# Column sums in column form, other instruction orders and two groups of constant products in an attention and ternary feed-forward kernel

## The chip, the cores and the metric

The kernel runs on one core of a Trainium2 chip. The metric is the device time of one execution in microseconds, as the median of three runs. The profile is one further execution, with its own time.

## The reference

For x of shape (8, 512, 256), each row is normalized (`xn`), and the output is `x + attention(xn) + ffn(xn)`. The core of it:

```python
q, k, v = split_heads(xn @ Wq), split_heads(xn @ Wk), split_heads(xn @ Wv)   # 16 heads of 16
scores = einsum('bhld,bhlwd->bhlw', q, k_win) * scale                        # window of 64 keys
ctx = einsum('bhlw,bhlwd->bhld', softmax(scores), v_win)
attention = ctx @ Wo

h = gelu(einsum('btd,hd->bth', xn, absmean(W_fc)))        # weights become -1, 0 or 1
h = layernorm(h, ln_w, ln_b)                              # over 1024 hidden values
ffn = einsum('bth,dh->btd', h, absmean(W_proj))
```

The layernorm is folded into the second product: with T the ternary `W_proj`, the kernel needs the two vectors of 256 sums `sum_h ln_w[h] T[d,h]` and `sum_h ln_b[h] T[d,h]`. The first is multiplied by each row's mean, the second is added to every row.

## The kernel before, in words

The eight batches go through the same jobs on TensorE (PE), each job ending in one semaphore. A job is named (batch, kind, number). Per batch there are: `xt` (8 transposes of xn), `qk` 0 and 1 (the q and k products, 12 of 512 columns each), `v` (24 of 256 columns), `fc` 0 to 3 (8 of 512 columns each), `sa` 0 to 7 (scores for the row maxima), `mt` (transposes of the maxima), `st` 0 to 7 (scores transposed, for the exponentials), `gt` 0 to 3 (8 transposes of the gelu output each), `proj` 0 to 3 (16 of 256 columns each), `pv` 0 to 7, `ct` 0 and 1 and `wo` 0 to 3. `sa` and `st` work on half of the array's rows at a time and begin with products that add the window mask from `mask_q`, `mask_k` and `onehot`; `sa` 0 of a batch is the first that reads the masks and the stacked copies of q and k.

PE takes the jobs in the order of the list ORDER, which is FIRST, then PERIOD repeated, then LAST, written out by hand as tables. Batches overlap: the exponentials and attention products of one batch stand between the q, k, fc and score jobs of the next. Results go to two rings of PSUM buffers, `big` (3 buffers: xt, qk, v, fc, sa, st, gt) and `small` (2 buffers, all others). A job waits until the job three (or two) places before it in its ring has been read out.

The other engines have orders of their own, written as lists of calls. ScalarE (ACT) rounds results to fp16 (`xt_hi`, `qk_split`, `g_hi`, `ct_hi`), does gelu (`gel`) and the exponentials (`probs`, `p_parts`). VectorE (DVE) makes the remainders (`xt_lo`, `qk_split`, `g_lo`, `ct_lo`), the maxima `negmax` (`maximum`, line 1016), the statistics of the hidden layer (`hidden_statistics`), and the sums of outputs. GpSimd (POOL) makes constants, masks and fillings at the start, and the remainders of the exponentials (`lower_part`, line 578). SyncE (SP) issues the DMAs: q and k go through `load_stack` as 12 DMAs per batch (line 374), the masks are copied to the second half of the partitions by `copy_masks` (lines 411 and 412).

The start of the program, on which much of the prediction rests:

- ACT sums |W_fc| (`absolute`, line 789); PE spreads the sum over the partitions (`sums`, line 1640). DVE takes the weights' maxima (line 1086), PE transposes them (`wmax`, line 1633), DVE writes `diag` (`largest`, lines 1096 and 1098), PE spreads it (`spread`, line 1636), and DVE makes scales from it.
- `xt` of batch 0 (line 1501), then DVE's `xt_lo` (line 992) and the 24 products of `qk` (line 1513).
- POOL fills `k_stack` with four memsets (lines 597 and 598).
- `crow` (line 1649): 48 products of 256 columns, with one column of `lnv_parts` as the stationary operand and T as the moving one. They leave the two vectors of sums in one row; `copy_row` (line 1152) copies it to `crow`, `csum` (line 1655) spreads it to 128 partitions, and `copy_sums` (line 1156) copies it to SBUF. POOL's `residual` and `add_mean` read it.

A batch's `gelu` t waits for the `hidden_statistics` t of the batch before.

Of the kernel before, what the change touches and what calls it, by code (L numbers as in the profile page):

```python
# [5 lines left out]
def attention_and_ternary_ffn(  # L6
# [53 lines left out]
    with ctx:  # L60
# [26 lines left out]
        crow = sb("crow", [1, 2 * D], fp32)  # L87
# [173 lines left out]
        def sig(name):  # L261
# [4 lines left out]
        FIRST = [(0, "wmax", 0), (0, "spread", 0), (0, "sums", 0), (0, "wmax", 1), (0, "xt", 0), (0, "spread", 1),  # L266
# [23 lines left out]
        PERIOD = [(3, "st", 0), (2, "pv", 6), (4, "fc", 0), (2, "ct", 0), (4, "fc", 1), (4, "fc", 2), (4, "fc", 3),  # L290
# [6 lines left out]
        LAST = [(5, "st", 0), (4, "pv", 6), (6, "fc", 0), (4, "ct", 0), (6, "fc", 1), (6, "fc", 2), (6, "fc", 3),  # L297
# [408 lines left out]
        def _(act):  # L706
# [91 lines left out]
            weight_upper(1)  # L798
            qk_upper(0, 1)
            gelu(0, 0)  # L800
            gelu(0, 1)
            gelu(0, 2)
            v_upper(0)
            normalize(1)
# [894 lines left out]
```

## Time and profile before

| | us |
|---|---|
| median of 3 runs | 398.52 |
| lowest and highest run | 396.35, 399.64 |
| profiled execution, its own time | 397.85 |
| its span, first to last instruction | 396.0 |
| PE busy | 373.7 (94%) |
| DVE busy | 321.2 (81%) |
| ACT busy | 287.6 (73%) |
| POOL busy | 231.4 (58%) |

The time of an execution is its span and 1.85 us around it. Matmuls are pipelined in the records: each lasts longer than the distance to the next. A wait on PE that is shorter than this overlap doesn't show as idle time, so the work on PE is read from the starts of the instructions and not from their durations.

### The profile page before, as it was taken

Reading aid. Unit: us, or ns where it says so; the run is one execution under the profiler, and the core shown is the slowest. Engines: PE = TensorE matmul, PEld = TensorE weight load, DVE = VectorE, ACT = ScalarE, POOL = GpSimd, SP = SyncE. Lnnn points to the kernel's source line nnn. Section 1 sums busy time; section 2 is a strip of 40 time slices with the busy share of each in tenths; the row PEclk is TensorE's granted clock in tenths of the full one; section 3 lists DMA queues with packets and bytes.
Section 4 is the critical chain, followed back from the end, with each engine's and each line's share of the span. In section 5 each row is a group of like instructions: output and inputs, shape, how many; then the busy total and the mean of one; then the engine's idle time right before and its main releaser. Section 6 shows DMA issues by size and latency. Waiting matters only on the chain.

```text
span 396.0 us, 13503 instructions
## 1 busy us (share of the span) xinstructions
PE 373.7 (94%) x5820; PEld 268.1 (68%) x5820; DVE 321.2 (81%) x645; ACT 287.6 (73%) x329; POOL 231.4 (58%) x186
## 2 busy tenths in 40 slices
PE   0698898999999999999999999999999999999995
PEld 0346565776577776876677775876677775778873
DVE  3898878699869998699959898599968898998555
ACT  2764249887986698767986698777977598768871
POOL 7901023866586548655576548655576647769871
PEclk9999989999999999999999999999999999999999
DMA  7459009600940267021910258021930256002002
GB/s 272 153 78 123 2 10 181 87 19 5 165 51 18 48 125 134 2 65 33 198 30 18 48 116 142 4 63 33 190 38 17 52 97 109 2 17 66 30 29 82
DMA packets 30685, 29.22 MB, mean 74 GB/s; under 512 B 5665, under 2 KB 29281, under 8 KB 30625
## 3 DMA queue, kind: packets, MB, share of 16 engines
q1 hardware_dynamic: 30624, 28.35, 36.6%
q8 instruction: 46, 0.75, 0.9%
q14 instruction: 15, 0.11, 0.1%
HBM read 7.35 MB, written 4.19 MB: 29 GB/s over the span
## 4 chain that ended last, share of the span: by engine, by line
PE 85%; DMA 4%; DVE 4%; ACT 3%; SPq 2%; issue 1%; POOL 1%; POOLq 1%; ACTq 0%
PE small L1600 15%; PE big L1539 13%; PE big L1513 11%; PE small L1611 10%; PE big L1590 7%; PE big L1578 5%; PE big L1553 5%; PE big L1525 5%; PE small L1627 5%; PE big L1583 4%; PE big L1559 4%; DMA mask_k<-mask_k 2%; SPq L374 2%; DMA gel<-in_w_fc 2%; PE small L1617 2%; PE big L1501 2%
## 5 line engine op out<-in xcount | busy, mean ns | idle before, releaser
L578 POOL TENSOR_TENSOR p_parts<-probs,p_parts 128x1024 f16<-128x1024 f32 x64 | 136.2, 2132 | 112.8 <-ACT p_parts L762 112.8
L761 ACT ACTIVATE probs<-big,exp_scale 128x1024 f32<-128x1024 f32 x64 | 71.4, 1116 | 22.9 <-PE big L1583 20.7
L1016 DVE TENSOR_REDUCE negmax<-big 128x8 f32<-128x1024 f32 x64 | 77.6, 1222 | 7.1 <-PE big L1559 5.7
L762 ACT ACTIVATE p_parts<-big,exp_scale 128x1024 f16<-128x1024 f32 x64 | 71.3, 1115 | 0.0
L1600 PE MATMUL small<-proj_t,g_hi 128*128 128x256 f16 x256 | 57.7, 273 | 0.0
L1600 PE MATMUL small<-proj_t,g_lo 128*128 128x256 f16 x256 | 57.5, 273 | 0.0
L776 ACT ACTIVATE g_hi<-big,lnw_s 128x512 f16<-128x512 f32 x64 | 39.8, 690 | 17.2 <-PE big L1590 17.2
L1539 PE MATMUL big<-fc_t,xt_hi 128*128 128x512 f16 x128 | 48.5, 379 | 1.0 <-DVE g_lo L1010 1.0
L1539 PE MATMUL big<-fc_t,xt_lo 128*128 128x512 f16 x128 | 48.6, 379 | 0.0
L1010 DVE SCALAR_TENSOR_TENSOR g_lo<-big,lnw_s,g_hi 128x512 f16<-128x512 f32 x64 | 46.5, 746 | 2.2 <-ACT g_hi L776 1.8
L749 ACT ACTIVATE gel<-big 128x1024 f32<-128x1024 f32 x32 | 32.7, 1025 | 12.6 <-PE big L1539 12.2
L1052 DVE SCALAR_TENSOR_TENSOR y_bufs<-small,rs,res 128x256 f32<-128x256 f32 x32 | 15.5, 483 | 30.6 <-PE small L1600 27.5
L1063 DVE TENSOR_TENSOR ctxn<-small,rden 64x128 f32<-64x128 f32 x128 | 36.9, 288 | 3.1
L1590 PE MATMUL big<-ident,gel 128*128 128x128 f32 x256 | 33.7, 280 | 0.0
L731 ACT ACTIVATE qk_split<-big 128x1024 f16<-128x1024 f32 x16 | 16.4, 1023 | 19.6 <-PE big L1513 19.1
L559 POOL TENSOR_TENSOR res<-x_in,csum 128x1024 f32<-128x1024 f32 x8 | 18.9, 2357 | 19.2 <-issue 19.2
L1590 PEld LDWEIGHTS big<-ident,gel 128*128 128x128 f32 x256 | 28.7, 143 | 1.5 <-DVE g_lo L1010 0.2
L1583 PEld LDWEIGHTS big<-q_stack,k_stack 50*128 50x128 f16 x1024 | 23.9, 94 | 7.6
L1553 PE MATMUL big<-mask_q,onehot 64*64 64x512 bf16 x256 | 26.0, 395 | 2.5 <-DMA mask_k<-mask_k 1.9
L1600 PEld LDWEIGHTS small<-proj_t,g_hi 128*128 128x128 f16 x256 | 25.0, 97 | 3.6
L1600 PEld LDWEIGHTS small<-proj_t,g_lo 128*128 128x128 f16 x256 | 25.0, 98 | 2.8
L1559 PEld LDWEIGHTS big<-k_stack,q_stack 48*64 48x64 f16 x1024 | 22.2, 106 | 6.3
(130 smaller groups left out, 812.2 us busy)
## 6 DMA issues: line engine op xcount, KB each, us to landing
q_stack<-qk_split SPq DMA_DIRECT2D x48, 128.0 KB, 4.0
k_stack<-qk_split SPq DMA_DIRECT2D x48, 128.0 KB, 5.3
x_in<-in_x SPq DMA_DIRECT2D x8, 512.0 KB, 5.5
out<-y_bufs SPq DMA_DIRECT2D x32, 128.0 KB, 2.4
v_odd<-v_even SPq DMA_DIRECT2D x16, 132.0 KB, 2.5
v_odd<-v_even SPq DMA_DIRECT2D x16, 99.0 KB, 2.2
gel<-in_w_fc SPq DMA_DIRECT2D x1, 1024.0 KB, 6.7
y_bufs<-in_w_proj SPq DMA_DIRECT2D x1, 1024.0 KB, 8.8
```

The costliest lines, as they stand in the source:

```text
L578: g.tensor_tensor(p_lo[:, (b * NJ + j) % PB], probs[:, (b * NJ + j) % PB], p_hi[:, (b * NJ + j) % PB], ALU.subtract).then_inc(*sig(p_lo_re ...
L761: s.activation(probs[:, (b * NJ + j) % PB].rearrange("p i (u q) -> p u i q", u=2), st, ACT.Exp, scale=exp_scale[:, 0:1]).then_inc(*sig(exp ...
L762: s.activation(p_hi[:, (b * NJ + j) % PB].rearrange("p i (u q) -> p u i q", u=2), st, ACT.Exp, scale=exp_scale[:, 0:1]).then_inc(*sig(p_hi ...
L776: s.activation(g_hi[:, i], slot[b, "gt", i // 2][:, i % 2], ACT.Copy, scale=lnw_s[:, i:i + 1]).then_inc(*sig(g_hi_ready))
L1010: v.scalar_tensor_tensor(out=g_lo[:, i], in0=slot[b, "gt", i // 2][:, i % 2], scalar=lnw_s[:, i:i + 1], in1=g_hi[:, i], op0=ALU.mult, op1= ...
L1016: v.tensor_reduce(negmax[:, :, j], slot[b, "sa", j][:].rearrange("p a (u k) -> p (a u) k", k=P), AX.X, ALU.max, negate=True).then_inc(*sig ...
L1513: last = mm(ps[:, m], wt[pw][:, n, k, m * P:(m + 1) * P], xt[px][:, k], start=(i == 0), stop=(i == 3 * KD - 1))
L1539: last = mm(ps[:, a], xt[px][:, k, n * P:(n + 1) * P], fc_t[:, k, a * L:(a + 1) * L], start=(i == 0), stop=(i == 2 * KD - 1))
L1553: mm(ps[a * W:(a + 1) * W, u], onehot[rows, a], mask_q[rows, 1 if n == 0 else 0].rearrange("p u k -> p (u k)"), start=True, stop=False)
L1583: last = mm(ps[:, u, i * W:(i + 1) * W], k_stack[rows, b % 2, i, n * W:n * W + P], q_stack[rows, b % 2, i, n], start=False, stop=(i == NP ...
L1590: last = nc.tensor.transpose(ps[:, a, t * P:(t + 1) * P], gel[:, t, (2 * n + a) * P:(2 * n + a + 1) * P], ident[:])
L1600: last = mm(ps[:, 0:D], gt[pg][:, i, n * P:(n + 1) * P], proj_t[:, i], start=(i == 0 and pg == 0), stop=(i == NH - 1 and pg == 1))
```

## The change

It has four parts.

1. The sums in column form. `crow` becomes 16 products: T's blocks of 128 x 128 are the stationary operand, the six columns of `lnv_parts` the moving one, and the sums come out in one column per vector and part. DVE adds the three parts (`ccol`, one reduction) and writes four diagonal blocks of 128 x 128 into `mean_term` (four operations with `ident`); `csum` then multiplies `ones` by these, two products of 256 columns.
2. Two jobs `warm` on PE: 6 products of 512 columns of `onehot` before the first `xt`, and 9 after `spread` 1, ahead of `qk` 0. They write the third `big` buffer, which nobody reads, and stand outside the ring. The second pair `wmax` 1 and `spread` 1 now stands together behind `xt`.
3. New tables for PE, and new lists for DVE, ACT, POOL and SP. Among the moves: `copy_masks` goes ahead of the first `load_stack`; `v` of batch 0 goes ahead of `fc` 2; `crow` goes from the place ahead of `sa` 0 to the one behind `sa` 3; `csum` goes from between `sa` 6 and 7 to between `gt` 2 and 3; `proj` 0 of batch 0 goes from between `fc` 0 and 1 of batch 1 to behind that batch's `v`; on DVE, the statistics of batch 0 and the copies of the sums move behind the maxima.
4. In the repeated stretch the same 47 jobs in another order; PERIOD now begins at `st` 3 and is repeated three times.

```diff
-        crow = sb("crow", [1, 2 * D], fp32)
+        ccol = sb("ccol", [P, KD, 2], fp32)
...
-        FIRST = [(0, "wmax", 0), (0, "spread", 0), (0, "sums", 0), (0, "wmax", 1), (0, "xt", 0), (0, "spread", 1),
...
+        FIRST = [(0, "wmax", 0), (0, "spread", 0), (0, "sums", 0), (0, "warm", 0), (0, "xt", 0), (0, "wmax", 1),
+                 (0, "spread", 1), (0, "warm", 1), (0, "qk", 0), (0, "qk", 1), (0, "sums", 1), (0, "fc", 0),
...
+            copy_masks()
             load_stack(0, 0, 0)
             load_stack(0, 0, 1)
             load_stack(0, 1, 0)
             load_stack(0, 1, 1)
-            copy_masks()
...
+            WARM = (6, 9)
...
+                if kind == "warm":
+
+                    if n == 0:
+                        pe.wait_ge(onehot_ready, 1)
+                    flat = onehot[:].rearrange("p i q -> p (i q)")
+                    for i in range(WARM[n]):
+                        mm(big[2][:, 1], flat[:, 0:P], flat, start=True, stop=True)
...
-                    for c in range(2):
-                        i = 0
+                    for h in range(KD):
                         for k in range(NH):
-                            for part in range(3):
-                                last = mm(ps[0:1, c * D:(c + 1) * D], lnv_parts[:, part, c, k:k + 1], proj_t[:, k],
-                                          start=(i == 0), stop=(i == 3 * NH - 1))
-                                i += 1
+                            last = mm(ps[:, h * 6:(h + 1) * 6], proj_t[:, k, h * P:(h + 1) * P],
+                                      lnv_parts[:, :, :, k], start=(k == 0), stop=(k == NH - 1))
...
-                    mm(ps[:], ones[0:1, :], crow[:], start=True, stop=True).then_inc(*sig(csum_done))
+                    for c in range(2):
+                        last = mm(ps[:, c * D:(c + 1) * D], ones[:], mean_term[:, c], start=True, stop=True)
+                    last.then_inc(*sig(csum_done))
...
-                v.tensor_copy(crow[:], slot[0, "crow", 0][0:1, :]).then_inc(*sig(crow_copied))
+                link_pre(v.tensor_reduce(ccol[:], slot[0, "crow", 0][:, 0:6 * KD].rearrange("p (h a c) -> p h c a", h=KD, c=2),
+                                         AX.X, ALU.add))
+
+                for c in range(2):
+                    for h in range(KD):
+                        last = v.tensor_scalar(mean_term[:, c, h * P:(h + 1) * P], ident[:], ccol[:, h, c:c + 1], None, ALU.mult)
+                last.then_inc(*sig(crow_copied))
```

On PE, at the start of the program, this stands in a row before (out<-stationary, moving operand's names; `red` is `wmax` or, with ones, `sums`; `diag` is `spread`):

```order
L1640 MATMUL small<-red,ones 128x1
L1633 MATMUL small<-ident,red 3x128
L1501 MATMUL big<-ident,xn 128x128 x8
L1636 MATMUL small<-diag,ones 128x3
L1513 MATMUL big<-xt_hi,w_hi 128x512
```

and this now:

```order
L1663 MATMUL small<-red,ones 128x1
L1519 MATMUL big<-onehot 128x512 x6
L1524 MATMUL big<-ident,xn 128x128 x8
L1656 MATMUL small<-ident,red 3x128
L1659 MATMUL small<-diag,ones 128x3
L1519 MATMUL big<-onehot 128x512 x9
L1536 MATMUL big<-xt_hi,w_hi 128x512
```

The transposes stand behind six added products, the transpose of the second maxima behind them, and the q products behind nine more.

On SP, before the first copies of q and k, the queue has this in a row before:

```order
L354 DMA x_in<-in_x 128x4x256
L374 DMA q_stack<-qk_split 16x8x512 x6
L374 DMA k_stack<-qk_split 16x8x512 x6
L411 DMA mask_q<-mask_q 64x1024
L412 DMA mask_k<-mask_k 64x256
L379 DMA v_odd<-v_even 64x792
```

and this now:

```order
L348 DMA x_in<-in_x 128x4x256
L405 DMA mask_q<-mask_q 64x1024
L406 DMA mask_k<-mask_k 64x256
L368 DMA q_stack<-qk_split 16x8x512 x6
L368 DMA k_stack<-qk_split 16x8x512 x6
L383 DMA q_stack<-mt 1x64x64 x4
L373 DMA v_odd<-v_even 64x792
```

The masks are ahead of the twelve copies, and the shifted values of v behind the maxima `mt`.

On DVE, between the last maxima of batch 0 and the last remainder `g_lo`, this stands in a row before:

```order
L1016 TENSOR_REDUCE negmax<-big 128x8 x3
L1010 SCALAR_TENSOR_TENSOR g_lo<-big,lnw_s,g_hi 128x512 x2
L1026 TENSOR_SCALAR mt<-small 128x64
L1027 SCALAR_TENSOR_TENSOR mt<-small,mt 128x64
L1156 COPY csum<-small 128x512
L997 TENSOR_TENSOR qk_split<-big,qk_split 128x2x512
L1010 SCALAR_TENSOR_TENSOR g_lo<-big,lnw_s,g_hi 128x512 x2
L997 TENSOR_TENSOR qk_split<-big,qk_split 128x2x512
L1010 SCALAR_TENSOR_TENSOR g_lo<-big,lnw_s,g_hi 128x512 x4
```

and this now:

```order
L1024 TENSOR_REDUCE negmax<-big 128x8 x2
L1018 SCALAR_TENSOR_TENSOR g_lo<-big,lnw_s,g_hi 128x512 x2
L1034 TENSOR_SCALAR mt<-small 128x64
L1035 SCALAR_TENSOR_TENSOR mt<-small,mt 128x64
L1160 TENSOR_REDUCE ccol<-small 128x4
L1165 TENSOR_SCALAR mean_term<-ident,ccol 128x128 x4
L1005 TENSOR_TENSOR qk_split<-big,qk_split 128x2x512
L1018 SCALAR_TENSOR_TENSOR g_lo<-big,lnw_s,g_hi 128x512 x2
L1005 TENSOR_TENSOR qk_split<-big,qk_split 128x2x512
L1018 SCALAR_TENSOR_TENSOR g_lo<-big,lnw_s,g_hi 128x512 x2
L1170 COPY csum<-small 128x512
L1018 SCALAR_TENSOR_TENSOR g_lo<-big,lnw_s,g_hi 128x512 x2
```

Five operations on the sums now stand ahead of the first `qk_split` of batch 1, and the copy of the sums ahead of the last two remainders.

## Rows read from the trace of the kernel before

**Rows 1.** Busy us (share of the span) and instructions of each engine.

```profile
PE 373.7 (94%) x5820; PEld 268.1 (68%) x5820; DVE 321.2 (81%) x645; ACT 287.6 (73%) x329; POOL 231.4 (58%) x186
```

**Rows 2.** Timeline of PE, two starts of `xt`: start, us, engine, line, operation.

```profile
127.59 1.09 PE L1501 MATMUL big<-ident,xn 128*128 128x128 f32 x8
...
172.33 1.09 PE L1501 MATMUL big<-ident,xn 128*128 128x128 f32 x8
```

**Rows 3.** Timeline at the start of the program, all engines, in order of time.

```profile
11.09 0.56 PE L1640 MATMUL small<-red,ones 128*128 128x1 f32 x2 [1.72 <-ACT scratch L789]
...
12.97 1.97 PE L1501 MATMUL big<-ident,xn 128*128 128x128 f32 x8 [0.69 <-ACT xn L715]
...
14.21 2.02 POOL L597 MEMSET k_stack<- 128x2304 uint32 x1
...
15.20 1.05 DVE L1098 TENSOR_SCALAR diag<-ident,wmax 3x3 f32<-3x3 f32 x1
...
16.03 1.22 DVE L992 TENSOR_TENSOR xt_lo<-big,xt_hi 128x1024 f16<-128x1024 f32 x1
...
16.67 2.02 POOL L597 MEMSET k_stack<- 128x2304 uint32 x1
17.17 2.60 DVE L1136 TENSOR_SCALAR p_parts<-gel,ntheta 128x2048 f16<-128x2048 f32 x1
...
17.31 0.61 PE L1513 MATMUL big<-xt_hi,w_hi 128*128 128x512 f16 x1 [0.36 <-DVE xt_lo L992]
```

**Rows 4.** Timeline of PE, three of the first q products.

```profile
21.12 0.64 PE L1513 MATMUL big<-xt_hi,w_hi 128*128 128x512 f16 x1
...
22.19 0.38 PE L1513 MATMUL big<-xt_hi,w_hi 128*128 128x512 f16 x1
...
22.41 0.38 PE L1513 MATMUL big<-xt_lo,w_hi 128*128 128x512 f16 x1
```

**Rows 5.** DMA issues between 30.4 and 32.5 us: KB each, us to landing.

```profile
k_stack<-qk_split SPq DMA_DIRECT2D x2, 128.0 KB, 8.0
...
mask_k<-mask_k SPq DMA_DIRECT2D x1, 32.0 KB, 8.1
```

**Rows 6.** Timeline of PE from `crow` to the first `proj`.

```profile
32.67 5.40 PE L1649 MATMUL small<-proj_t,lnv_parts 128*1 128x256 f16 x48
39.96 0.41 PE L1553 MATMUL big<-mask_q,onehot 64*64 64x512 bf16 x4 [1.89 <-DMA mask_k<-mask_k]
...
49.37 1.97 PE L1590 MATMUL big<-ident,gel 128*128 128x128 f32 x8
```

**Rows 7.** Windows: us, PE, PEld, DVE, ACT, POOL busy, granted clock, DMA share, GB/s.

```profile
48.60:50.00 1.40, 1.40 (x24) 1.08 (x24) 1.40 (x2) 0.00 (x0) 0.00 (x0) 0.64 0.00 0
50.00:52.40 2.40, 2.40 (x10) 1.52 (x9) 1.88 (x3) 1.03 (x2) 0.00 (x0) 0.50 0.00 0
```

**Rows 8.** Timeline of DVE around the idle time behind the first maxima.

```profile
48.09 3.48 DVE L1016 TENSOR_REDUCE negmax<-big 128x8 f32<-128x1024 f32 x3
...
59.47 1.22 DVE L997 TENSOR_TENSOR qk_split<-big,qk_split 128x1024 f16<-128x1024 f32 x1 [1.11 <-ACT qk_split L731]
```

**Rows 9.** Timeline of PE, `st`, `sa`, `sa`, `pv`, `proj` in a row.

```profile
164.59 0.39 PE L1578 MATMUL big<-onehot,mask_k 64*128 64x512 bf16 x2
...
165.15 0.41 PE L1553 MATMUL big<-mask_q,onehot 64*64 64x512 bf16 x4
...
165.61 0.39 PE L1553 MATMUL big<-mask_q,onehot 64*64 64x512 bf16 x4
...
166.16 0.77 PE L1611 MATMUL small<-v_even,p_parts 128*128 128x33 f16 x24
166.77 0.27 PE L1600 MATMUL small<-proj_t,g_hi 128*128 128x256 f16 x1
```

**Rows 10.** Chain that ended last, from 380 us on.

```profile
381.31 1.11 ACT probs L761
...
383.51 2.13 POOL p_parts L578
```

More of the change, by code:

```diff
@@ L262, in sig @@
             return PER[name][0], PER[name][2]
-        FIRST = [(0, "wmax", 0), (0, "spread", 0), (0, "sums", 0), (0, "wmax", 1), (0, "xt", 0), (0, "spread", 1),
[23 rows of a table removed]
-        PERIOD = [(3, "st", 0), (2, "pv", 6), (4, "fc", 0), (2, "ct", 0), (4, "fc", 1), (4, "fc", 2), (4, "fc", 3),
[6 rows of a table removed]
-        LAST = [(5, "st", 0), (4, "pv", 6), (6, "fc", 0), (4, "ct", 0), (6, "fc", 1), (6, "fc", 2), (6, "fc", 3),
[17 rows of a table removed]
-        ORDER = FIRST + [(p + ahead, kind, n) for p in range(2) for ahead, kind, n in PERIOD if p + ahead < NB] + LAST
+        FIRST = [(0, "wmax", 0), (0, "spread", 0), (0, "sums", 0), (0, "warm", 0), (0, "xt", 0), (0, "wmax", 1),
[19 rows of a table added]
+        PERIOD = [(2, "st", 3), (3, "sa", 3), (2, "pv", 1), (2, "proj", 2), (3, "sa", 4), (2, "st", 4), (1, "wo", 0),
[6 rows of a table added]
+        LAST = [(5, "st", 3), (6, "sa", 3), (5, "pv", 1), (5, "proj", 2), (6, "sa", 4), (5, "st", 4), (4, "wo", 0),
[15 rows of a table added]
+        ORDER = FIRST + [(p + ahead, kind, n) for p in range(3) for ahead, kind, n in PERIOD if p + ahead < NB] + LAST
         READ_OUT = {"xt": xt_ready, "qk": qk_ready, "v": v_ready, "fc": gelu_ready, "sa": max_ready,
@@ L325, in attention_and_ternary_ffn @@
         for ring, is_big in ((big, True), (small, False)):
-            jobs = [j for j in ORDER if (j[1] in IN_BIG) == is_big]
+            jobs = [j for j in ORDER if (j[1] in IN_BIG) == is_big and j[1] != "warm"]
             for i, j in enumerate(jobs):
@@ L643, in _ @@
             add_mean(1)
-            lower_part(1, 1)
-            token_rstd(3)
-            lower_part(1, 2)
-            lower_part(1, 3)
-            lower_part(1, 4)
-            lower_part(1, 5)
-            residual(2)
-            for p in range(3):
+            for p in range(4):
+                token_rstd(p + 3)
+                lower_part(p + 1, 1)
+                lower_part(p + 1, 2)
+                lower_part(p + 1, 3)
+                lower_part(p + 1, 4)
+                lower_part(p + 1, 5)
+                residual(p + 2)
                 lower_part(p + 1, 6)
@@ L855, in _ @@
             exp(1, 5)
-            context_upper(0, 1)
             gelu_upper(2, 0)
             gelu_upper(2, 1)
-            for p in range(3):
-                qk_upper(p + 3, 0)
-                exp(p + 1, 6)
-                gelu_upper(p + 2, 2)
-                gelu_upper(p + 2, 3)
-                exp(p + 1, 7)
-                qk_upper(p + 3, 1)
-                gelu_upper(p + 2, 4)
-                gelu_upper(p + 2, 5)
-                gelu_upper(p + 2, 6)
-                gelu_upper(p + 2, 7)
-                exp(p + 2, 0)
-                gelu(p + 3, 0)
-                context_upper(p + 1, 0)
-                gelu(p + 3, 1)
-                gelu(p + 3, 2)
-                gelu(p + 3, 3)
-                exp(p + 2, 1)
-                v_upper(p + 3)
-                exp(p + 2, 2)
-                exp(p + 2, 3)
-                normalize(p + 4)
+            qk_upper(3, 0)
+            context_upper(0, 1)
+            exp(1, 6)
+            gelu_upper(2, 2)
+            gelu_upper(2, 3)
+            exp(1, 7)
+            qk_upper(3, 1)
+            gelu_upper(2, 4)
+            gelu_upper(2, 5)
+            gelu_upper(2, 6)
+            gelu_upper(2, 7)
+            exp(2, 0)
+            context_upper(1, 0)
+            gelu(3, 0)
+            gelu(3, 1)
+            gelu(3, 2)
+            gelu(3, 3)
+            exp(2, 1)
+            v_upper(3)
+            exp(2, 2)
+            exp(2, 3)
+            normalize(4)
+            for p in range(2):
                 exp(p + 2, 4)
@@ L883, in _ @@
                 exp(p + 2, 5)
-                context_upper(p + 1, 1)
                 gelu_upper(p + 3, 0)
                 gelu_upper(p + 3, 1)
+                qk_upper(p + 4, 0)
+                context_upper(p + 1, 1)
+                exp(p + 2, 6)
+                gelu_upper(p + 3, 2)
+                gelu_upper(p + 3, 3)
+                exp(p + 2, 7)
+                qk_upper(p + 4, 1)
+                gelu_upper(p + 3, 4)
+                gelu_upper(p + 3, 5)
+                gelu_upper(p + 3, 6)
+                gelu_upper(p + 3, 7)
+                exp(p + 3, 0)
+                context_upper(p + 2, 0)
+                gelu(p + 4, 0)
+                gelu(p + 4, 1)
+                gelu(p + 4, 2)
+                gelu(p + 4, 3)
+                exp(p + 3, 1)
+                v_upper(p + 4)
+                exp(p + 3, 2)
+                exp(p + 3, 3)
+                normalize(p + 5)
+            exp(4, 4)
+            xt_upper(6)
+            exp(4, 5)
+            gelu_upper(5, 0)
+            gelu_upper(5, 1)
             qk_upper(6, 0)
+            context_upper(3, 1)
             exp(4, 6)
@@ L1184, in _ @@
             maximum(0, 4)
+            maximum(0, 5)
             xt_lower(1)
-            maximum(0, 5)
             maximum(0, 6)
@@ L1335, in _ @@
                 v_lower(p + 4)
+                maximum(p + 4, 0)
                 add_projection(p + 3, 1)
-                maximum(p + 4, 0)
+                maximum(p + 4, 1)
                 scale_context(p + 3, 0)
-                maximum(p + 4, 1)
+                maximum(p + 4, 2)
                 scale_context(p + 3, 1)
-                maximum(p + 4, 2)
+                maximum(p + 4, 3)
+                maximum(p + 4, 4)
                 add_projection(p + 3, 2)
-                maximum(p + 4, 3)
+                maximum(p + 4, 5)
@@ L1374, in _ @@
             hidden_statistics(6, 1)
+            hidden_statistics(6, 2)
+            scale_context(4, 7)
             statistics(7)
-            context_lower(4, 0)
-            scale_context(4, 7)
             add_projection(5, 0)
             v_lower(6)
+            maximum(6, 0)
             add_projection(5, 1)
-            maximum(6, 0)
+            maximum(6, 1)
             scale_context(5, 0)
-            maximum(6, 1)
+            maximum(6, 2)
             scale_context(5, 1)
-            maximum(6, 2)
+            maximum(6, 3)
@@ L1413, in _ @@
             gelu_lower(6, 6)
             gelu_lower(6, 7)
+            scale_context(5, 6)
             hidden_statistics(6, 3)
-            scale_context(5, 6)
+            context_lower(5, 0)
+            add_attention(4, 3)
             hidden_statistics(7, 0)
             hidden_statistics(7, 1)
-            context_lower(5, 0)
+            hidden_statistics(7, 2)
             scale_context(5, 7)
-            hidden_statistics(7, 2)
             hidden_statistics(7, 3)
+            maximum(7, 0)
@@ L1423, in _ @@
             add_projection(6, 0)
             add_projection(6, 1)
-            maximum(7, 0)
+            maximum(7, 1)
             scale_context(6, 0)
-            maximum(7, 1)
+            maximum(7, 2)
             scale_context(6, 1)
-            maximum(7, 2)
+            maximum(7, 3)
             add_projection(6, 2)
-            maximum(7, 3)
+            maximum(7, 4)
             add_attention(5, 0)
-            maximum(7, 4)
             maximum(7, 5)
             scale_context(6, 2)
+            maximum(7, 6)
@@ L1492, in _ @@
             ps_hl = (p_hi, p_lo)
+            WARM = (6, 9)
             def job(b, kind, n):
-                ps = slot[b, kind, n]
-                wait_slot(pe, (b, kind, n))
-                if kind == "xt":
+                if kind != "warm":
+                    ps = slot[b, kind, n]
+                    wait_slot(pe, (b, kind, n))
+                if kind == "warm":
[4 more added lines that the diff above has]
+                        mm(big[2][:, 1], flat[:, 0:P], flat, start=True, stop=True)
+                elif kind == "xt":
                     pe.wait_ge(*at(b, xn_ready, 1))
```

290 lines of the change are left out of this document (136 added, 154 removed), and 85 rows, old and new, of tables (FIRST, LAST, PERIOD).

## The prediction

> **What bounds the kernel now.** I read the busy shares first, then PE's timeline batch by batch, then the start and the end of the program. PE is busy for 373.7 of 396.0 us, DVE for 321.2 [rows 1]. That alone would leave 22 us to win, so the question is where PE waits.
>
> In the repeated stretch it doesn't. `xt` of one batch starts at 127.59 and that of the next at 172.33, so a batch takes 44.74 us [rows 2]. The same 47 jobs priced by the distance between their starts give 42.3 us: 8 products of 256 columns at 0.109 us each for every half `proj`, and so on. The rest is explained by one thing. Two `sa` in a row stand 0.46 us apart (165.15, 165.61), but an `st` followed by an `sa` 0.56 us (164.59, 165.15) [rows 9]. So each change between kinds of job that use different rows of the array costs 0.095 us, and PERIOD has 27 of them: 2.6 us. 42.3 + 2.6 is 44.9, the measured period. Nothing waits there, and a new order can gain nothing in it except by fewer such changes.
>
> What is lost, is lost at the ends. At the start, the first q product is at 17.31, and nine products later it is 21.12: 0.42 us each. Those at 22.19 and 22.41 are 0.22 apart [rows 3, 4]. These are the two levels of TensorE's clock, 1.2 and 2.4 GHz. The profile's clock column misses this first slow stretch. Then `crow` runs until 38.07 (32.67 + 5.40), and PE stands idle for 1.89 us, until the copy of the masks has landed, just before 39.96 [rows 6]. The eight `sa` that follow go at the pace of DVE's maxima (three in 3.48 us [rows 8]), PE waits in between, and the granted clock falls: 0.64 from 48.60 to 50.00, 0.50 from 50.00 to 52.40 [rows 7]. Everything that PE does between about 49.0 and 52.4 takes twice its time, the first `gt` (49.37 [rows 6]) included: half of 3.4 us, some 1.5 us, is lost. At the end, the last exponential (381.31) and the two POOL remainders behind it set the chain [rows 10].
>
> **The change part by part**, against the profiled execution's own 397.85 us.
>
> *Warm products.* They add 15 products and no result, so they can pay only through the clock. The first group begins behind `sums` at 11.65 (11.09 + 0.56), and 6 x 0.427 us later it is 14.2. The transposes stood at 12.97, so they start 1.2 us late and end at about 16.1 instead of 14.94 [rows 3]. `xt_lo` ended 2.31 us behind them (16.03 + 1.22 = 17.25), so it is there at 18.4. The second group starts behind `spread` at about 17.4. If the clock is up by then, it takes 9 x 0.216 = 1.9 us and q starts at 19.4; if not, 3.8 us and q starts at 21.3. In exchange, the 12 products of `qk` 0 take 12 x 0.216 = 2.6 us instead of 4.9 (17.31 to 22.19, where `qk` 1 begins [rows 3, 4]). The first q result is ready at 22.0 in the good case, against 22.2 before, and at about 24 in the bad one. I take the clock to be up in most executions, and the net to be +0.1 us, with -0.9 and +1.8 as ends. A group of filler that delays the real work by as much as it saves gains nothing.
>
> *Masks first.* The last copies of k, issued from 30.4 to 31 us, take 8.0 us to land, so they are there at about 38.7; the masks, issued behind them, take 8.1, and release `sa` 0 at 39.96 [rows 5, 6]. With the masks issued before q is computed, while the queue is empty, `sa` 0 waits for k alone: 1.2 us earlier at least. The masks (128 and 32 KB, as much as one and a quarter of the twelve copies) and the shifted v are no longer among the copies; that is worth up to another 1 us, an estimate from the 8 us that a copy of 128 KB takes in this crowd. I take -1.5 (-1.2 to -2.2).
>
> *`crow` in column form.* 48 products of 5.40 us leave, 16 small ones come. The nearest row is `pv`: 24 products with a fresh 128 x 128 operand in 0.61 us (166.16 to 166.77) [rows 9], so 0.4 us; the upper end is 16 of 256 columns, 1.75 us. But the 5.4 us lay in front of a wait, and PE reaches `sa` 0 before its data in both kernels. Without `crow`, and with `v` and `fc` 2 done at about 33.2, PE stands idle for about 5 us instead of 1.89. The gain of 5.0 us of work is zero on the path. Its new place, behind `sa` 3, is in DVE's shadow too.
>
> *The longer idle stretch has a price.* Before, the clock held through 1.89 us of idleness and fell only at about 49, behind sparse work. Five idle us may well let it fall before `sa` 0. Then `sa` 0, `sa` 1 and the 8 products of `fc` 3 (1.73 us at the high clock) take twice as long, and the third maximum, on which all DVE's further ones hang, comes up to 2.5 us later. Ends 0 and +2.5; I take +1.5.
> The Trainium skill, "TensorE: Matmul & The Clock Gate", section "Loop structure matters more than you think", says that a long DMA wait between matmuls makes PE go cold. No row of before shows a DMA wait that did: after 1.89 us the products were still fast. By the page the sum would carry the full +2.5, by the row 0.
>
> *Copy of the sums, `csum` and the moved statistics.* The reduction and four small products on DVE, about 1.0 us (an estimate: each has a quarter of the elements of a g_lo or less, and the ends are 0.7 and 1.3), stand ahead of `qk_split` 0 of batch 1. DVE waited 1.11 us for ACT ahead of the next `qk_split` [rows 8], which hides them. `csum` itself (1.05 us) stood between two `sa`, in a gap; now it stands between `gt` 2 and 3 where PE is nearly gapless, delays `g_hi` of the last `gt`, the first exponential and with it `fc` 2 of batch 1. Part of it fills short waits that PE has there. +0.6, between 0 and +1.5.
>
> *Orders.* From `st` 0 of batch 0 to the end I count 201 changes of row kind before and 210 after: in the tables, 27 and 28 per repeated stretch, the rest at the ends. 9 x 0.095 = +0.85 us, with nothing to hide it. I followed the new period's waits for buffers with these durations (exponential pair 2.2 us, 381.31 to 383.51 [rows 10]; a third of 3.48 us for a maximum, 1.22 for the remainder of q [rows 8]): the tightest, `qk` 1 behind the exponential of `st` 6, has 0.5 us to spare. So 44.8 us per batch.
>
> *The end.* The last exponential pair but one now waits for `st` 6 instead of `pv` 3, both at about the same place, and the chain of ACT, POOL, `pv` 7, `ct` 1 and `wo` behind it is the same. 0.
>
> The sum: 0.1 - 1.5 + 1.5 + 0.6 + 0.85 = +1.5, so 397.85 + 1.5 = 399.3 us. The profiled execution was 0.7 us faster than the median of 398.52, and the slow stretch at its start was short; the new kernel should depend less on this luck, so I leave the 0.7 out.
>
> **The rivals.**
>
> *DVE is shut out by POOL (slower).* `diag` 3x3 is a tiny operation, but at 15.20 it took 1.05 us and ended at 16.25, when POOL's memset (14.21 + 2.02) was over; `p_parts` at 17.17 took 2.60 us, half of it until the memset from 16.67 ended at 18.69 [rows 3]. In the new order the `wmax` transpose comes behind the transposes, at about 16.0, so its maximum is read by 16.7 and `diag` asks for memory at 16.7, just as POOL starts the second long memset. If it loses, `diag` is done at 18.75 instead of 16.8. `xt_lo` stands behind it: 20.0. `spread`, the nine products (by then at the low clock, 3.8 us) and q follow: q starts at 23.0, with its first products slow as well, and its first result comes at about 26 instead of 22.3. +3.7 us: 403.0. From about 0.1 us of lateness on it decides. Against it: if the clock rises during the transposes, `diag` comes 0.2 us or more before the memset.
> The Trainium skill, "SBUF — State Buffer", section "Who interferes with whom", says that a `tensor_scalar` in a two-port mode and a GpSimd instruction hold a shared port for the whole instruction, and that the later one waits in full. The two rows agree with it.
>
> *The clock stays up (faster).* If it rises during the first group and holds through the wait before `sa` 0, the transposes are shorter, q comes 0.7 us earlier, the 1.5 us for the slow scores fall away, and with luck 0.9 of the 1.5 us around `gt` 0: 399.3 - 3.1 = 396.2. For it: the clock held through 1.89 us. Against: 5 us is much more, and the scores leave PE as idle as before.
>
> *The warm products don't lift the clock in time.* A group, transposes and a gap may not count as steady work: 1.97 us of transposes from 12.97 on didn't raise it before q [rows 3, 4]. Then the second group takes 3.8 us: +1.8 for the start, 401.1.
>
> **How the numbers follow.** The forecast has a chance of 0.42, the shut-out of DVE 0.22, the clock that stays up 0.22, the useless warm products 0.14. The predicted time is 399.3. The likeliest case's own range is 397.5 to 401. The range of all is 396.0 to 403.2, the clock's good case to the shut-out. One per cent, 4 us, is about what a measurement of this kernel can tell from no change: the limits are 394.5 and 402.5. All cases but the shut-out lie inside; of this one (and its mixtures with the slow scores) 0.17 is beyond 402.5. For faster I leave 0.11: the good case together with copies that land a full 2.2 us earlier. That leaves 0.72.
>
> **What would show it.** Right: `xt` starts at 14.2 and its last transpose ends by 16.1; `sa` 0 starts at 38 to 38.8; no idle time on PE between `fc` of batch 1 and `st` 7 of batch 7; 44.8 us between `xt` of batches 3 and 4; the granted clock below 1 once near 40 and once near 50. Wrong: q's first product before 18.5 or behind 22; `diag` longer than 1 us (then the shut-out); products of `sa` 0 and `fc` 3 at the 2.4 GHz spacing (then the good case); a period other than 44.7 to 44.9 (then my reading that the order has nothing to give is wrong); the last exponential elsewhere in the chain at the end.

## The result and the profile after

The changed kernel takes 415.75 us (median of 4 runs, 410.66 to 421.94) against 398.24 us of the kernel before, measured beside it. The ratio is 1.036, with a 95% interval of 1.0254 to 1.0466; all ratios leave out executions more than 1.5% above the fastest one of their kernel, here 417.28 and 421.94 us. I had predicted 399.3 us and a range of 396.0 to 403.2. That is wrong by far more than any term of my sum.

The profiled execution took 414.23 us, its span is 412.4. First the busy times (they answer to [rows 1]), and the shares of the span of the chain that ended last, from the page of the changed kernel:

```profile
PE 375.3 (91%) x5805; PEld 267.0 (65%) x5805; DVE 323.8 (78%) x649; ACT 288.2 (70%) x329; POOL 231.6 (56%) x186
...
PE 65%; DMA 12%; SPq 11%; ACT 4%; issue 4%; DVE 3%; POOL 1%; POOLq 1%; ACTq 0%
```

The same shares in the kernel before:

```profile
PE 85%; DMA 4%; DVE 4%; ACT 3%; SPq 2%; issue 1%; POOL 1%; POOLq 1%; ACTq 0%
```

The engines work about as long as before. What is new is that DMA and SP's queue have 23% of the chain, against 6%. The next view is PE's timeline, two starts of `xt` (batches 3 and 4) and all waits for a DMA behind the start, those of `sa` 0 of batches 3 to 7:

```profile
128.47 1.09 PE L1524 MATMUL big<-ident,xn 128*128 128x128 f32 x8
164.38 0.41 PE L1576 MATMUL big<-mask_q,onehot 64*64 64x512 bf16 x4 [1.05 <-DMA k_stack<-qk_split]
174.53 1.09 PE L1524 MATMUL big<-ident,xn 128*128 128x128 f32 x8
210.40 0.41 PE L1576 MATMUL big<-mask_q,onehot 64*64 64x512 bf16 x4 [1.01 <-DMA k_stack<-qk_split]
257.44 0.41 PE L1576 MATMUL big<-mask_q,onehot 64*64 64x512 bf16 x4 [2.02 <-DMA k_stack<-qk_split]
304.34 0.58 PE L1576 MATMUL big<-mask_q,onehot 64*64 64x512 bf16 x4 [1.88 <-DMA k_stack<-qk_split]
351.40 0.41 PE L1576 MATMUL big<-mask_q,onehot 64*64 64x512 bf16 x4 [3.05 <-DMA k_stack<-qk_split]
```

From `xt` of batch 3 to that of batch 4 it is 46.06 us now, against 44.74 [rows 2], and `sa` 0 of every batch from 3 on waits for the last copy of k. Before, PE never waited there. The windows show what such a wait costs besides (columns as in [rows 7]):

```profile
33.00:38.00 5.00, 0.04 (x4) 0.07 (x7) 2.59 (x7) 0.04 (x1) 1.71 (x4) 0.68 0.79 82
38.00:42.00 4.00, 4.00 (x47) 2.06 (x48) 2.36 (x2) 0.00 (x0) 0.00 (x0) 0.55 0.00 0
42.00:60.00 18.00, 16.16 (x233) 10.62 (x231) 15.24 (x22) 10.15 (x15) 0.00 (x0) 1.00 0.08 19
304.00:308.00 4.00, 3.66 (x34) 2.56 (x35) 1.23 (x1) 0.62 (x1) 2.13 (x1) 0.57 0.09 22
351.00:356.00 5.00, 4.60 (x56) 2.99 (x56) 2.10 (x3) 0.29 (x1) 2.58 (x2) 0.66 0.00 0
```

Behind the idle stretch from 33 to 38 the granted clock is 0.55, and the same happens behind the waits of 1.88 and 3.05 us (0.57 and 0.66). Up to `xt` of batch 2 the changed kernel is only 1 us behind (86.49 against 85.50). Of the 16.4 us between the spans, 15.4 are lost after it.

Why k is late, SP's queue tells. This is the timeline of SP in the kernel before, from the maxima of batch 2 to the copies of batch 3:

```profile
137.70 2.68 SPq L389 DMA_DIRECT2D q_stack<-mt  x4
140.48 2.52 SPq L374 DMA_DIRECT2D q_stack<-qk_split  x4
144.24 0.37 SPq L395 DMA_DIRECT2D out<-y_bufs  x1
144.71 0.39 SPq L354 DMA_DIRECT2D x_in<-in_x  x1
145.14 1.20 SPq L374 DMA_DIRECT2D q_stack<-qk_split  x2
146.38 1.79 SPq L395 DMA_DIRECT2D out<-y_bufs  x2
148.22 3.78 SPq L374 DMA_DIRECT2D k_stack<-qk_split  x6
```

And this the same stretch of the changed kernel:

```profile
138.73 3.16 SPq L383 DMA_DIRECT2D q_stack<-mt  x4
145.99 0.99 SPq L389 DMA_DIRECT2D out<-y_bufs  x2
147.08 4.37 SPq L368 DMA_DIRECT2D q_stack<-qk_split  x6
151.55 0.54 SPq L348 DMA_DIRECT2D x_in<-in_x  x1
152.13 3.85 SPq L368 DMA_DIRECT2D k_stack<-qk_split  x6
```

The half of q that was ready near 140 isn't issued at 140.48 but at 147.08. The stores 1 and 2 of batch 0 stand ahead of it, and they wait for `wo` 1 and 2 and DVE's sums. Then twelve copies of 0.6 us each follow each other, with `load_x` between them, and those of k are issued 3.9 us later than before. The chain that ended last passes just there:

```profile
144.78 1.32 PE small L1650 x12
...
146.13 0.49 DVE y_bufs L1088
...
146.64 0.33 SPq L389
...
155.38 8.86 DMA k_stack<-qk_split
```

The last piece is a second part of the lateness: this copy takes 8.86 us from issue to landing. The median of all 48 copies of k, from the DMA issues of the page, is 8.2 us, against 5.3 before. Why they land more slowly is not shown.

### The profile page after: what moved, and what is told of

Same layout as the page of the kernel before. It is cut to its first block, busy times and chain, and to the rows that moved or that the text cites. A ratio compares the mean times of both kernels' runs of the same rounds, so it can differ in the third digit from the quotient of the medians.

```text
span 412.4 us, 13477 instructions
## 1 busy us (share of the span) xinstructions
PE 375.3 (91%) x5805; PEld 267.0 (65%) x5805; DVE 323.8 (78%) x649; ACT 288.2 (70%) x329; POOL 231.6 (56%) x186
## 4 chain that ended last, share of the span: by engine, by line
PE 65%; DMA 12%; SPq 11%; ACT 4%; issue 4%; DVE 3%; POOL 1%; POOLq 1%; ACTq 0%
PE small L1623 13%; DMA k_stack<-qk_split 11%; PE big L1536 10%; SPq L368 9%; PE small L1634 8%; PE big L1576 5%; PE big L1613 4%; PE big L1562 4%; PE big L1601 4%; PE small L1650 4%; PE big L1582 3%; PE big L1606 3%; PE big L1548 3%; PE big L1524 2%; DMA gel<-in_w_fc 2%
## 5 line engine op out<-in xcount | busy, mean ns | idle before, releaser
L1623 PE MATMUL small<-proj_t,g_hi 128*128 128x256 f16 x256 | 60.2, 280 | 0.0
L1623 PE MATMUL small<-proj_t,g_lo 128*128 128x256 f16 x256 | 60.1, 280 | 0.0
L1018 DVE SCALAR_TENSOR_TENSOR g_lo<-big,lnw_s,g_hi 128x512 f16<-128x512 f32 x64 | 44.6, 745 | 0.4
L1576 PE MATMUL big<-mask_q,onehot 64*64 64x512 bf16 x256 | 26.9, 409 | 17.7 <-DMA k_stack<-qk_split 9.0
L730 ACT ACTIVATE gel<-big 128x1024 f32<-128x1024 f32 x32 | 31.8, 1024 | 15.2 <-PE big L1562 14.8
L1613 PE MATMUL big<-ident,gel 128*128 128x128 f32 x256 | 32.8, 275 | 0.7 <-DVE xt_lo L1000 0.7
L1060 DVE SCALAR_TENSOR_TENSOR y_bufs<-small,rs,res 128x256 f32<-128x256 f32 x32 | 15.4, 482 | 17.0 <-PE small L1623 16.8
L1582 PEld LDWEIGHTS big<-k_stack,q_stack 48*64 48x64 f16 x1024 | 23.2, 109 | 6.6 <-issue 0.8
L712 ACT ACTIVATE qk_split<-big 128x1024 f16<-128x1024 f32 x16 | 16.4, 1024 | 15.1 <-PE big L1536 15.0
```

The lines of the kernel that those rows point to most:

```text
L1018: v.scalar_tensor_tensor(out=g_lo[:, i], in0=slot[b, "gt", i // 2][:, i % 2], scalar=lnw_s[:, i:i + 1], in1=g_hi[:, i], op0=ALU.mult, op1= ...
L1576: mm(ps[a * W:(a + 1) * W, u], onehot[rows, a], mask_q[rows, 1 if n == 0 else 0].rearrange("p u k -> p (u k)"), start=True, stop=False)
L1613: last = nc.tensor.transpose(ps[:, a, t * P:(t + 1) * P], gel[:, t, (2 * n + a) * P:(2 * n + a + 1) * P], ident[:])
L1623: last = mm(ps[:, 0:D], gt[pg][:, i, n * P:(n + 1) * P], proj_t[:, i], start=(i == 0 and pg == 0), stop=(i == NH - 1 and pg == 1))
```

## The experiments

Each ran beside the kernel before on the same chip; ratios are to it. In the first four its median was 396.92 us, in the next four 398.1, in the following three 398.16, in the last four 398.05. None leaves a part of the computation out; what added products write is never read.

**Stores behind the copies.** In the changed kernel, in SP's list for every batch from 3 on:

```diff
-            store(0, 1)
-            store(0, 2)
             load_stack(3, 0, 0)
...
             load_stack(3, 1, 1)
+            store(0, 1)
+            store(0, 2)
```

> The changed kernel with its SP list alone edited: the two stores of output blocks 1 and 2 of each batch go from ahead of the next q and k copies to behind them. Theory (SP's queue is held by a store that waits for the last output products, so the copies of q and k start some 5 us late in every batch): the waits of PE for k_stack at the first sa of batches 3 to 7 (9.0 us in all) vanish, the distance of the xt jobs goes from 46 to 48.5 back to 44.8, the clock no longer falls behind 300 us, and the time is 398 to 400.5. Rival 1 (the copies are slow because the 512 KB load of x stands between q's and k's): the waits stay at half or more, 405 to 412. Rival 2 (the new order of PE waits somewhere by itself): the waits for DMA go and others come, 405 or more.

403.3 us, ratio 1.0136 (1.0089 to 1.0182). All waits for k from batch 3 on are gone, `xt` comes every 44.95 us, and 2.2% of the 3.6% are back, by the ratios. Most of the loss is this one place in SP's list. The copies of k still take 8.4 us to land (median), so their slower landing does not by itself make PE wait.

**The same stores put ahead in the kernel before** (`store(1, 1)` and `store(1, 2)` ahead of `load_stack(4, 0, 0)`, and so on).

> The kernel before with its SP list alone edited: the stores of blocks 1 and 2 go ahead of the next batch's q and k copies from batch 3 on, as in the changed kernel. Theory (SP's queue): q's first copy of a batch starts about 6 us later, behind the wo products, and k's last one with it, so PE waits before the first sa of batches 3 to 7; its sa 0 is one proj later in its order than in the changed kernel, so the waits are smaller: 400 to 407. Rival 2 (PE's own order is what costs): no change, 397 to 399.

401.2 us, 1.0096 (1.0066 to 1.0125): slower, but by less than half of the 2.2%. On the old order only one wait for k shows in PE's timeline, 1.27 us at 342.43. There `sa` 0 comes later in PE's list, behind `proj` 1. The new order of PE took this slack away, and the new list of SP needed it. The copies of k also land sooner there, 6.9 us against 8.2, and no run separates the two.

**`load_x` behind the copies too.**

> As the first of this call, and the load of x of the next but one batch also goes behind the copies of k. Theory (SP's queue, stores alone): same as that kernel within 1 us. Rival 1 (load of x among the copies): faster than it by 2 us or more, since k's copies land in 5 instead of 8 us.

405.15 us, 1.0171 (1.0115 to 1.0226): nothing won, so `load_x` between the copies is not what costs.

**Without the warm products** (stores behind, `WARM` groups taken out).

> As the first of this call, without the two groups of constant products. Theory of the prediction: the groups delay the transposes by 1.2 us and give back as much at q, so the time is the same within 1 us. Rival (they pay): without them 1.5 to 3 us slower, q's first products at the 1.2 GHz spacing. Rival (they cost): 1 us faster or more.

404.44 us, 1.0172 (1.0137 to 1.0208), q at 18.00 but slow at first (0.43 us from product to product). Without the groups it takes 1.1 us more by the medians and 1.4 by the ratios, which the intervals don't tell from nothing.

**The new start alone** (new lists of every engine up to the last `gt` of batch 0, then the old ones), **and the new orders alone** (old start, then the new lists with the stores behind).

> The new start (masks first, warm products, sums in column form, new order of every engine up to the last gt of batch 0), then the old order of everything from st 0 of batch 0 on. The kernel with the stores behind the copies is still 6.4 us over the kernel before (403.3 to 396.9). Theory A, the rest is made by the orders behind the start: this kernel then stands within 1.5 us of before, 396 to 398.5. Theory B, the rest is made at the start (a wait of 6 us before sa 0, slow scores and a slow fc 3 behind it): then it comes to 401 to 404.

> The old start and old sums, then from st 0 of batch 0 on the new orders, with the stores 1 and 2 behind the copies. The counterpart of the start alone. Theory A (orders): 401 to 403.5, made of the wait of 2.2 us before sa 0 of batch 1, 0.2 us more per batch, and 1.5 us in the last stretch. Theory B (start): 397 to 399. If the two parts add up, its excess and that of the start alone make 6.4 us.

401.16 us, 1.0077 (1.0045 to 1.011), and 399.03 us, 1.0047 (1.0026 to 1.0069). They multiply to 1.0124, near the measured 1.0136: both theories had a part, the start probably the larger (the intervals overlap). The new orders' part shows in the trace of the second as 0.7 us between `xt` of batches 2 and 7 (221.76 against 221.06), and 1.5 us in the last stretch: from `xt` 7 on 91.6 against 89.44 us, of which 0.6 is the `pv` 2 that now stands behind it. In this execution the clock was 1.00 near 50 us, and `xt` of batch 2 came 1.9 us earlier than in the profile before (83.64 against 85.50); so its whole span is only 1.0 us longer.

**The parts of the start, each on the kernel before.** Masks first:

```diff
             load_x(1)
+            copy_masks()
             load_stack(0, 0, 0)
...
             load_stack(0, 1, 1)
-            copy_masks()
```

> The kernel before with only the two DMAs of the masks moved ahead of the first copies of q and k. My prediction gave this move 1.2 to 2.2 us. Theory: sa 0 of batch 0 starts at 38.2 to 38.8 instead of 39.96, its idle time shrinks from 1.9 to under 1 us, and the time falls by 1.2 us to some 395.7. Rival: the copies of k land no earlier than the masks did, because the 16 DMA engines share the same bytes and the queue is drained at the same moment; then no change, 396.9, or DVE's maxima are late anyway and hide it.

394.74 us, 0.9916 (0.9892 to 0.9941). It wins 3.4 us, more than I gave it, and is faster than both kernels. Of the 20 executions of the kernel before that ran beside it, the five with a mean granted clock of 1.0 have a median of 396.8 us, the others 398.14. By this some 2.1 us are the earlier `sa` 0 and the rest is the clock near 50. Columns alone:

> The kernel before with only the sums in column form, in the old places of every order. PE has 5 us less to do before sa 0 and waits longer for the masks, about 6.5 us. Theory (a long idle stretch costs the clock): granted clock about 0.5 to 0.6 for 4 us from sa 0 on, sa 0, sa 1 and fc 3 at twice their time, +1 to +2.5 us: 398 to 399.5. Rival (the score jobs go at DVE's pace anyway): within 0.5 us of 396.9.

400.7 us, 1.0067 (1.0044 to 1.009). The windows of the two, masks first and columns:

```profile
46.00:48.00 2.00, 1.92 (x29) 1.14 (x28) 2.00 (x3) 0.00 (x0) 0.00 (x0) 1.00 0.00 0
48.00:50.00 2.00, 1.96 (x12) 0.89 (x10) 2.00 (x3) 1.26 (x2) 0.00 (x0) 1.00 0.00 0
50.00:52.00 2.00, 2.00 (x20) 1.14 (x18) 1.28 (x5) 0.83 (x1) 0.00 (x0) 1.00 0.04 8
```

```profile
36.00:38.00 2.00, 0.00 (x0) 0.00 (x0) 1.74 (x7) 1.32 (x3) 0.51 (x2) 0.50 1.14 125
38.00:40.00 2.00, 0.00 (x0) 0.00 (x0) 0.00 (x0) 0.75 (x2) 0.00 (x0) 0.50 0.79 142
42.00:44.00 2.00, 2.00 (x9) 0.72 (x6) 1.60 (x2) 0.00 (x0) 0.00 (x0) 0.50 0.00 0
```

With the masks first PE works on `crow` until `sa` 0 starts, at 37.83 instead of 39.96, and the clock stays up through 48 to 52, where it fell before [rows 7]. With the columns PE waits 7.19 us for the masks, and the granted clock is 0.50 until 44. Both together, every order as before:

> The kernel before with the masks first and the sums in column form, every order else as before. Alone, the masks gave -3.4 us (ratio 0.9916) and the columns +2.6 (1.0067). Theory (the 5.4 us of crow kept the clock up through the wait for the copies): the copies now release sa 0 near 37.8, but PE has stood idle for 5 us, the granted clock is 0.5 at sa 0, and the gain of the masks is mostly lost: 0.998 to 1.002 of before. Rival (the two don't interact, or crow costs time itself once the masks are early): 0.9916 or less.

399.31 us, 1.0035 (1.0011 to 1.0058): the columns undo the masks' gain, 4.6 us. Then the same with 24 products in the wait whose results nobody reads:

```diff
                     if n == 0:
+                        if b == 0:
+                            for i in range(24):
+                                mm(ps[:, 1], flat[:, 0:P], flat, start=True, stop=True)
                         pe.wait_ge(*at(b // 2, stacks_loaded[b % 2], 12))
```

> The kernel before with masks first and column sums (399.31, ratio 1.0035), and 24 products of constants ahead of sa 0. Theory (the idle stretch, not the column form, costs the time): granted clock 1.00 from 33 to 46, and the time of the kernel with the masks first alone, 394.5 to 395.5, ratio 0.991 to 0.993: 24 useless products win 4 us. Rival (something in the column form costs time, such as the diagonal blocks on DVE): at most 1 us is won.

396.15 us, 0.9961 (0.9941 to 0.9981). The granted clock of the profile is 1.00 in the whole execution (its column misses the first slow q products here too). 3.2 of the 4.6 us are back, so they were the clock. The other 1.4 us are the copies of k: with the masks alone `crow` was the last thing that `sa` 0 waited for (37.83), here it was k (39.20). Its copies were issued 0.3 us later, from 27.10 instead of 26.80, and landed in 7.5 us instead of 6.7 (medians of the six). In every profile with the sums in column form the first six copies of k take 7.5 us or more, in every one with the old sums 6.7 to 7.2. Why the column form slows them is not known.

**The filler in the changed kernel**, with the stores behind.

> The changed kernel with the stores behind the copies (403.3, ratio 1.0136), and 24 products of constants (5.2 us at the high clock) added directly ahead of sa 0, in the wait for the copies; they write the buffer that sa 0 then starts anew. Theory (the idle 6 us cost the clock): the granted clock stays at 1.00 from 33 to 50, sa 0, sa 1 and fc 3 run at full speed, xt of batch 1 comes 2 to 3 us earlier, and the time falls by 2 to 3 us: ratio 1.006 to 1.009. Rival (the slow scores are hidden behind DVE's maxima, or the clock falls for another reason): no change, 1.0136.

403.65 us, 1.0118 (1.0066 to 1.017), its runs 399.54, 403.26, 404.04 and 404.16. The clock does stay up (38 to 42 in the windows):

```profile
38.00:42.00 4.00, 3.96 (x19) 1.58 (x17) 2.39 (x5) 0.00 (x0) 1.70 (x4) 1.00 0.97 97
```

From `sa` 0 to `xt` of batch 2 it takes 45.86 us instead of 48.67. That the median hardly moves has another reason, to be seen in the timeline of this execution near 16 us:

```profile
14.10 1.91 PE L1524 MATMUL big<-ident,xn 128*128 128x128 f32 x8
16.27 0.28 DVE L1104 TENSOR_REDUCE wmax<-small 3x1 f32<-3x128 f32 x1 [1.22 <-PE small L1660]
16.43 2.02 POOL L591 MEMSET k_stack<- 128x2304 uint32 x1
16.58 1.89 DVE L1106 TENSOR_SCALAR diag<-ident,wmax 3x3 f32<-3x3 f32 x1
18.62 0.56 PE L1663 MATMUL small<-diag,ones 3*128 3x3 f32 x2 [2.39 <-DVE diag L1106]
19.11 4.02 PE L1519 MATMUL big<-onehot 128*128 128x512 bf16 x9
22.92 0.63 PE L1536 MATMUL big<-xt_hi,w_hi 128*128 128x512 f16 x1
```

Here the same in the changed kernel's own profile:

```profile
11.66 2.72 PE L1519 MATMUL big<-onehot 128*128 128x512 bf16 x6
14.17 1.11 PE L1524 MATMUL big<-ident,xn 128*128 128x128 f32 x8
15.75 0.57 DVE L1106 TENSOR_SCALAR diag<-ident,wmax 3x3 f32<-3x3 f32 x1
16.73 2.02 POOL L591 MEMSET k_stack<- 128x2304 uint32 x1
18.70 0.38 PE L1536 MATMUL big<-xt_hi,w_hi 128*128 128x512 f16 x1
```

The transposes at 14.1 took 1.11 us there and 1.91 here. So `diag` came ahead of the second memset there, and beside it here, and `spread` began 2.2 us later (18.62 against 16.46). The nine products behind it then ran at the low clock, 4.02 us instead of 2.12, and q began 4.2 us later in all. This is my rival of the shut-out, which I had priced at 3.7 us. It showed in the profiles of three kernels (`load_x` behind too, start alone, this one), not in two others with the same groups. The Trainium skill, "SBUF — State Buffer", section "Who interferes with whom", says that a `tensor_scalar` in a two-port mode and a GpSimd instruction exclude each other for the whole instruction; the two rows end together (18.47 and 18.45) and agree.

**`wmax` 1 back ahead of the first warm group**, and in addition **`load_x(2)` behind the copies of batch 1**.

> The kernel with the stores behind and 24 products ahead of sa 0 (403.65, its runs 399.54 and 403.26 to 404.16), and wmax 1 back ahead of the first warm group, so that diag no longer depends on when the transposes end. Theory (DVE is shut out by POOL's second memset in most executions): diag is done by 16.3 in every execution, the first q product comes at 18 to 19.5, and all runs lie near 399.5, ratio 1.002 to 1.005. Rival (the spread of 4 us comes from the clock in the first 20 us, whatever diag does): runs at 403 to 404 remain.

> The same, and load_x(2) moved behind the copies of k of batch 1 in SP's queue. Theory (load_x(2) waits for the residual of batch 0, which waits for the csum that the change moved 5 us later; the k copies of batch 1 stand behind it): the k copies of batch 1 are issued about 1 us earlier, the wait of 1.3 to 2.2 us before sa 0 of batch 1 falls under 0.5 us, and the time falls by 1 to 1.5 us against the run without this move. Rival (the copies are late because q and k themselves are late, or land late because x_in shares the DMA engines with them): the wait stays above 1 us, no change.

401.56 us, 1.0102 (1.0076 to 1.0129), runs from 400.91 to 402.38: the spread is gone and `diag` takes 0.22 us. The level is 2 us above what I expected. In its trace `wmax` 1 waits 1.78 us for the second maxima, which the new DVE list has late, and the group and `xt` wait behind it (`xt` at 17.31); `sums` ahead of it was 1.1 us late too in this execution. The second: 404.56 us, 1.017 (1.0139 to 1.0201), 3 us slower. These are timelines of it, of PE and DVE:

```profile
75.22 0.41 PE L1580 MATMUL big<-mask_q,onehot 64*64 64x512 bf16 x4
...
79.11 0.28 PE L1627 MATMUL small<-proj_t,g_hi 128*128 128x256 f16 x1 [3.25 <-DVE ctxn L1071]
```

```profile
76.51 1.40 DVE L989 BATCH_NORM_STATS2 bn<-x_in 128x6 f32<-128x256 f32 x4 [5.68 <-DMA x_in<-in_x]
```

The wait at `sa` 0 of batch 1 (1.51 us without the move) is gone, as the theory had it. But `x_in` lands later, DVE's statistics wait 5.68 us for it, and `proj` behind them. Neither of the two orders removes the loss. `load_x(2)` waits for POOL's residual, and this for the copy of `csum`: in the changed kernel the copy begins at 60.50, the residual at 61.31, and `x_in` is issued at 63.85; before it was 55.23, 56.04 and 60.48. But the late `csum` alone explains little of the wait. In the changed kernel the six copies of q fill the queue until 63.75 anyway, so it holds `x_in`, and k behind it, for 0.1 us; in the kernel with `wmax` 1 moved back, for 0.9 us (64.29 to 65.18). No run moved `csum` back by itself.

**Fillers that delay nothing**, on the kernel with the masks first: 4, 1 and 4 products where PE stands idle at the start, then five more ahead of `sa` 4 to 7.

> The kernel with the masks first (394.74) and nine constant products in places where PE stands idle at the start: 4 ahead of the first sums, 1 ahead of the first xt, 4 behind it. Unlike the added groups of the changed kernel they delay nothing. Theory: the clock is up when q begins, the first nine q products take 0.22 us each instead of 0.42, and the time falls by 1 to 1.8 us, to 393 to 393.7. Rival: q's products are fast, but what follows is set by the issue of the twelve copies (3.8 us for six) and by DVE, so under 0.5 us comes out; second rival: the gaps between the fillers keep the clock low and nothing changes.

> The kernel with the masks first and nine products in the gaps of the start (394.82; its trace: first q product fast, but a granted clock of 0.55 from 46 to 50), and five more products in the waits ahead of sa 4 to 7 of batch 0. Theory: the clock then holds through 46 to 50 and the 0.9 us won by a fast q come through: 393.3 to 393.8, ratio 0.987 to 0.989. Rival: the products are in the way of the scores, or the clock falls all the same: 394.5 to 395.5.

394.82 us, 0.9912 (0.9877 to 0.9947), and 393.73 us, 0.9907 (0.9886 to 0.9927). A window of each, the first, then the second:

```profile
46.00:48.00 2.00, 1.92 (x24) 1.76 (x14) 2.00 (x3) 0.00 (x0) 0.00 (x0) 0.55 0.00 0
```

```profile
46.00:48.00 2.00, 2.00 (x31) 1.41 (x31) 2.00 (x3) 0.00 (x0) 0.00 (x0) 1.00 0.04 8
```

The first made all q products fast and gave it back in a slow stretch at 46; the second holds the clock. The gain of the second over the masks alone is 1 us, within the intervals; the first gains nothing. The masks first are what beats both kernels; the rest is small.

## Why the prediction was wrong

- *The step that failed is "Orders".* I "followed the new period's waits for buffers" and gave it 44.8 us per batch. I followed PSUM buffers, ACT, DVE and POOL, and not SP's queue, although the diff showed `store(0, 1)` and `store(0, 2)` moved ahead of `load_stack(3, 0, 0)`. Measured: 46.0 to 48.5 us per batch, with PE waiting 1.0 to 3.1 us for k in each; moving the stores back gave 2.2% of the time, by far the largest term. Even with the stores behind, the period is 44.95 and the last stretch 1.5 us longer: the orders cost 1.9 us by the ratio of the run with them alone, not 0.85, and "the end: 0" was wrong.
- *The start as a whole.* My four terms for it add up to +0.7 us; alone it measured 1.0077, some +3.1.
- *Masks first, -1.5.* Right in sign, too small: 3.4 us. `sa` 0 came 2.1 us earlier, near my upper end of 2.2; I hadn't seen that the clock can then stay up near 50; its mean was 1.0 in all four executions.
- *`crow` in column form, 0, and the idle stretch, +1.5.* The mechanism was right: `sa` 0 at 37.96 (38 to 38.8 foreseen), clock 0.55 near 40. The size was not: 2.6 us alone and 4.6 us on top of the masks, of which 3.2 are the clock and 1.4 copies of k that land later. The old products were filler that did useful work. I had the masks' and the columns' effects side by side in a sum, though both act through the same wait. The Trainium skill, "TensorE: Matmul & The Clock Gate", section "Loop structure matters more than you think", says that a long DMA wait between matmuls makes PE go cold. The traces agree: the granted clock is 0.50 to 0.55 after waits of 5.99, 6.20 and 7.19 us ahead of the first `sa` 0. It is 0.57 after the 1.88 us at 304, while the 1.89 us in the kernel before left it at 1.00.
- *`csum`, +0.6.* I asked what it delays on PE, not who reads it: its reader's reader is `load_x(2)`, ahead of k in SP's queue. `sa` 0 of batch 1 waits 2.22 us in the changed kernel. The profile names ACT, but the exponential that ended then (76.94) is that of `st` 2, which `sa` 0 need not wait for, and in the run with `load_x(2)` behind k the wait is gone; so it is k. How much of it `csum` makes stays open: 0.1 us of queue, by the trace. The copies of v, of which this stretch of SP's list now has four instead of two, and the slower landing (8.5 us against 7.6 before) are in it too, and were not tried apart.
- *Warm products, +0.1.* q at 18.70, even ahead of my good case (19.4), because the transposes were fast already. The rival that DVE is shut out is real, in some executions and not in others; q comes some 4 us later then. It is not what made the kernel slow: the profiled execution of 414.23 us did not have it.
- *A second drop of the clock near 50* did not come (1.00 from 42 to 60).

## What to carry to other kernels

A queue that issues DMAs in order is an engine like any other. When a list moves, ask of each entry what it waits for and which entries behind it are already due: a store that waits for the end of one batch must not stand ahead of the copies that start the next. Before taking work away from PE ahead of a wait, ask what the clock does in the longer wait; and price edits that shorten and fill the same wait together.

## What was not expected

- 24 products that nobody reads made a kernel 3.2 us faster (399.31 to 396.15).
- Between executions of one kernel the transposes behind the same six products took 1.11 or 1.91 us, the clock having risen or not. Through `diag`, the memset and nine products at the low clock this becomes 4 us at q.
- The waits of 1.05, 1.01 and 2.02 us at 164, 210 and 257 left the clock at 1.00, those of 1.88 and 3.05 us at 304 and 351 did not. Two windows of the changed kernel, directly ahead of the wait at 304 and of that at 257:

```profile
299.40:302.40 3.00, 3.00 (x41) 2.37 (x39) 0.90 (x7) 2.28 (x3) 2.37 (x6) 1.00 1.18 115
252.40:255.40 3.00, 3.00 (x41) 2.35 (x38) 1.78 (x9) 2.25 (x3) 0.12 (x1) 1.00 1.08 121
```

PE worked without a gap ahead of both, so neither the length of the wait nor the work just ahead of it tells them apart. What does stays open.
